# Three products at a time taken from VectorE's last scans by GpSimd, between its gathers, and a second accumulator bank

## What is computed

```python
# mamba branch (d_inner 512, 16 states)
xz = xn @ in_proj.T;  x, z = split(xz);  x = silu(causal_conv4(x) + conv_b)
dt, Bm, Cm = split(x @ x_proj.T);  dt = softplus(dt @ dt_proj.T + 2 * dt_proj_b)
h[t] = exp(dt * A) * h[t-1] + dt * Bm[t] * x[t]          # 16 states for each of 512 channels
y = (sum over states of h * Cm + x * D) * z;  return y @ out_proj.T
# moe branch: 64 experts, the 8 best of each token, hidden 256, inner 128
h = silu(x @ w1_e.T) * (x @ w3_e.T);  out += weight * (h @ w2_e.T)
```

## Time and profile before

| | us |
|---|---|
| three runs | 499.99, 503.32, 513.6 |
| median | 503.32 |
| the profiled execution | 495.79 |
| its span on the core | 494.0 |
| VectorE busy in the span | 432.0 (87%) |
| TensorE busy | 410.0 (83%) |
| GpSimd busy | 327.0 (66%) |
| ScalarE busy | 248.2 (50%) |
| mean granted TensorE clock | 0.906 |

### The profile page before, as it was taken

One profiled execution on the slowest core, in us unless ns is written; L12 is line 12 of the kernel. 1 busy time (PEld: TensorE's weight loads), 2 busy tenths in 40 slices (PEclk: granted clock), 3 DMA queues, 4 the chain that ended last, 5 costly groups with the idle time before them and its releaser, 6 DMA issues. The chain is left out here.

```text
span 494.0 us, 8730 instructions
## 1 busy us (share of the span) xinstructions
PE 410.0 (83%) x2094; PEld 299.1 (61%) x2094; DVE 432.0 (87%) x651; ACT 248.2 (50%) x469; POOL 327.0 (66%) x281
## 2 busy tenths in 40 slices
PE   1986989018859999899999998899989849865997
PEld 1732434002229888788978886788878735533675
DVE  5297999989997998999889997999899899999984
ACT  1245269132335566566666674556656522554560
POOL 2000578777767788878865665878877687778770
PEclk9997899655558999999999998999999988995999
DMA  8999389962234999999999996999999663333331
GB/s 274 428 425 426 138 297 400 407 244 106 101 144 159 347 376 374 354 322 357 346 365 329 338 359 234 347 340 353 363 349 336 247 202 93 101 113 105 113 117 53
DMA packets 51849, 134.39 MB, mean 272 GB/s; under 512 B 7120, under 2 KB 11216, under 8 KB 49776
## 3 DMA queue, kind: packets, MB, share of 16 engines
q1 hardware_dynamic: 45680, 117.31, 65.1%
q0 software_dynamic: 6144, 16.79, 10.3%
HBM read 90.49 MB, written 45.68 MB: 276 GB/s over the span
## 5 line engine op out<-in xcount | busy, mean ns | idle before, releaser
L344 POOL TENSOR_TENSOR dbu<-dtu,bc 128x512 f32 x80 | 102.7, 1286 | 57.3 <-DVE bank L600 46.4
L336 POOL DMA_INDIRECT slot_x<-x_sb,slot x64 | 69.3, 1082 | 68.5 <-DMA slot_x<-bc 49.3
L600 DVE TENSOR_TENSOR_SCAN bank<-dA,dbu 128x512 f32<-128x512 f32 x68 | 92.6, 1362 | 8.9 <-POOL dbu L344 1.3
L786 ACT ACTIVATE dA<-dt_sb,a_neg 128x512 f32<-128x512 f32 (+1 forms) x68 | 49.2, 725 | 68.2 <-DVE bank L600 68.1
L600 DVE TENSOR_TENSOR_SCAN bank<-bank,dbu 128x512 f32<-128x512 f32 x60 | 73.7, 1229 | 5.3
L1034 PE MATMUL bank<-x_sb,wring 128*128 128x128 f32 x528 | 67.9, 284 | 0.0
L606 DVE TENSOR_TENSOR hc<-bank,bc 128x512 f32<-128x512 f32 x90 | 61.8, 687 | 5.2 <-POOL hp L354 3.2
L1034 PEld LDWEIGHTS bank<-x_sb,wring 128*128 128x128 f32 x528 | 65.0, 200 | 0.3
L1034 PE MATMUL bank<-x_sb,xw 128*128 128x128 f32 x512 | 62.6, 275 | 0.7 <-DMA xw<-w_moe 0.7
L1034 PEld LDWEIGHTS bank<-x_sb,xw 128*128 128x128 f32 x512 | 59.7, 192 | 1.2 <-issue 1.2
L786 ACT ACTIVATE bank<-dt_sb,a_neg 128x512 f32 x60 | 41.6, 693 | 35.1 <-DVE bank L600 35.0
(11 more groups left out here) (175 smaller groups left out, 735.8 us busy)
## 6 DMA issues: line engine op xcount, KB each, us to landing
xw<-w_moe SPq DMA_DIRECT2D x64, 384.0 KB, 5.4
wring<-w_moe SPq DMA_DIRECT2D x64, 384.0 KB, 5.4
slot_y<-x_sb SPq DMA_DIRECT2D x66, 256.0 KB, 5.5
slot_x<-bc SPq DMA_DIRECT2D x16, 1024.0 KB, 21.9
bc<-bc_dram SPq DMA_DIRECT2D x8, 1024.0 KB, 15.5
xg<-slot_x SPq DMA_DIRECT2D x16, 512.0 KB, 6.0
xw<-slot_x SPq DMA_DIRECT2D x16, 512.0 KB, 6.1
slot_y<-w_moe SPq DMA_DIRECT2D x1, 2048.0 KB, 13.7
```

The source lines that it names most:

```text
L336: pool.indirect_dma_start(slot_x, bass.IndirectOffsetOnAxis(ap=slot[:, t * K + k:t * K + k + 1], axis=0), x_sb[:, t, :], None).then_inc(sc ...
L344: nc.gpsimd.tensor_tensor(dbu[:, j], at(dtu, g), bc[:, bass.ds(n, 1), 0].rearrange("p a l -> p (a l)"), ALU.mult).then_inc(dbu_ok, 1)
L600: nc.vector.tensor_tensor_scan(H[:], dA[:, j] if fall is None else fall, dbu[:, j], 0.0, ALU.mult, ALU.add).then_inc(scan_ok, 1)
L786: nc.scalar.activation(dA[:, j] if fall is None else fall, at(dt_sb, g), ACT.Exp, scale=a_neg[:, bass.ds(g, 1), bass.ds(n, 1)].rearrange(" ...
```

## The change

Four parts.

1. GpSimd leaves group 5 after its state 11. The products `spread_u` of states 12 to 15 of group 5 are made by VectorE, `times_c` of these states writes four buffers of their own (`hc_alone`), and TensorE adds them one by one with `sum_states`; GpSimd makes neither their products nor their `add_pair`.
2. GpSimd's 64 gathers start after that, and are interrupted twice: in front of gather 22 it makes the products of states 13, 14, 15 of group 6, in front of gather 44 those of states 10, 11, 12 of group 7. They go to four buffers `extra`; VectorE makes no `spread_u` for these six states and reads `extra` in the scan.
3. Group 6 is summed in a bank of its own (`PS[1]`); group 7 in `Y_ACC`, whose first sum then waits for `finish_group` of group 5. `finish_group` of group 6 now stands behind six states of group 7. The table `PROJ` and the output banks are laid out anew.
4. The SBUF reserved for GpSimd's DMA descriptors (`dynamic_dma_scratch_size`) is set to 8192 bytes a partition, where it had its default of 16384; `extra` takes 8 KB a partition.

```diff
+        extra = sb("extra", [P, 4, L])
+        hc_alone = [f[:].rearrange("p t e -> p (t e)") for f in (prob, key)] + [
+            wx[:].rearrange("p t n -> p (t n)")[:, 0:L], hp[:]]
-        OUT = [PS[i][:, 0:DM] for i in (4, 5, 6, 7, 1, 2, 4, 5)]
+        OUT = [PS[i][:, 0:DM] for i in (4, 5, 6, 7, 2, 4, 5, 6)]
-        PROJ = {9: (4, 0), 11: (4, 1), 13: (5, 0), 15: (5, 1), 21: (6, 0), 23: (6, 1), 25: (7, 0), 26: (7, 1),
-                27: (4, 2), 28: (5, 2), 29: (6, 2), 30: (7, 2)}
+        PROJ = {9: (4, 0), 10: (4, 1), 20: (5, 0), 21: (5, 1), 24: (6, 0), 25: (6, 1), 26: (4, 2), 27: (5, 2),
+                28: (7, 0), 29: (7, 1), 30: (6, 2), 31: (7, 2)}
+        def acc_of(g):
+            return PS[1] if g == G2 else Y_ACC
+        ALONE = NS - 4
+        PAUSE = {22: ((G2, 13), (G2, 14), (G2, 15)), 44: ((G3, 10), (G3, 11), (G3, 12))}
+        BY_POOL = [s for group in PAUSE.values() for s in group]
...
-            with pool.Fori(DT, G2) as g:
+            with pool.Fori(DT, G2 - 1) as g:
                 with pool.Fori(0, QG // 2) as q:
                     pairs(g, q)
-            add_pair((G2 - G1) * QG - 1, 1)
+            with pool.Fori(0, ALONE // 4) as q:
+                pairs(G2 - 1, q)
+            r = (G2 - 1 - G1) * QG + ALONE // 2 - 1
+            add_pair(r, 1)
+            def ahead(g, n):
+                i = BY_POOL.index((g, n))
+                if i >= 4:
+                    pool.wait_ge(scan_ok, BY_POOL[i - 4][0] * NS + BY_POOL[i - 4][1] + 1 + C)
+                nc.gpsimd.tensor_tensor(extra[:, i % 4], dtu[:, g], bc[:, n, 0], ALU.mult).then_inc(dbu_ok, 1)
...
                 for k in range(K):
+                    for g, n in PAUSE.get(t * K + k, ()):
+                        ahead(g, n)
                     pool.indirect_dma_start(
...
-            def light(g, p):
+            def light(g, p, alone=False):
...
                         scan(g, n, k % 2, dA_light(n))
+                        if alone and ALONE - 1 <= n < NS - 1:
+                            spread_u(g, n + 1, 1 - k % 2)
...
+            light(G2 - 1, (G2 - GH - 2) * LIGHT + V_LAST, alone=True)
...
+            def tail_pair(g, q):
+                for j in range(2):
+                    n = 2 * q + j
+                    if n % PART == 0 and (n >= RING or g == G3):
+                        dve.wait_ge(acc_ok, g * NS + n - RING + PART + C)
+                    s = (g - G2) * NS + n
+                    if (g, n) in BY_POOL:
+                        i = BY_POOL.index((g, n))
+                        dve.wait_ge(dbu_ok, DBU_MOE + i + 1)
+                        scan(g, n, j, given=extra[:, i % 4])
+                    else:
+                        dve.wait_ge(dbv_ok, NS + NS - ALONE + s + 1 - sum((h - G2) * NS + m < s for h, m in BY_POOL))
+                        scan(g, n, j)
+                    after = (g, n + 1) if n < NS - 1 else (g + 1, 0)
+                    if after[0] < G and after not in BY_POOL:
+                        spread_u(after[0], after[1], 1 - j)
+                    times_c(g, n, j, hc_end)
...
-                if n == 0:
-                    pe.wait_ge(y_out, g + 1)
+                if n == 0 and g == G2:
+                    pe.wait_ge(scan_ok, G2 * NS + C)
+                elif n == 0:
+                    pe.wait_ge(y_out, min(g + 1, G2 + 1))
...
-            sum_quad((G2 - G1) * (NS // 4) - 1)
+            for n in range(ALONE, NS):
+                sum_states(G2 - 1, n, hc_alone, 1)
...
-    nc = bacc.Bacc("TRN2", target_bir_lowering=False, num_devices=1)
+    nc = bacc.Bacc("TRN2", target_bir_lowering=False, num_devices=1, dynamic_dma_scratch_size=8192)
```

More of the change, by code:

```diff
@@ L594, in spread_u, with scan @@
                                         ALU.mult).then_inc(dbv_ok, 1)
-            def scan(g, n, j, fall=None):
+            def scan(g, n, j, fall=None, given=None):
                 s = g * NS + n
@@ L599, in scan @@
                 dve.wait_ge(hc_ok, s + C)
-                nc.vector.tensor_tensor_scan(H[:], dA[:, j] if fall is None else fall, dbu[:, j], 0.0, ALU.mult, ALU.add).then_inc(scan_ok, 1)
+                nc.vector.tensor_tensor_scan(H[:], dA[:, j] if fall is None else fall, dbu[:, j] if given is None else given, 0.0, ALU.mult, ALU.add).then_inc(scan_ok, 1)
             def times_c(g, n, j, ring=None):
@@ L607, in times_c, with finish_group @@
                                         ALU.mult).then_inc(hc_ok, 1)
-            def finish_group(g):
+            def finish_group(g, bank=None):
                 dve.wait_ge(acc_ok, (g + 1) * NS + C)
-                nc.vector.scalar_tensor_tensor(at(u_g, g), at(u_g, g), at(d_col, g), Y_ACC[:], ALU.mult, ALU.add).then_inc(y_out, 1)
+                nc.vector.scalar_tensor_tensor(at(u_g, g), at(u_g, g), at(d_col, g), (bank or Y_ACC)[:], ALU.mult, ALU.add).then_inc(y_out, 1)
                 dve.wait_ge(y_out, g + 2)
@@ L656, in light @@
                         n = 4 * c + k
-                        dve.wait_ge(dbu_ok, (g - G1) * NS + n + 1)
+                        own = alone and n >= ALONE
+                        if own:
+                            dve.wait_ge(dbv_ok, NS + n - ALONE + 1)
+                        else:
+                            dve.wait_ge(dbu_ok, (g - G1) * NS + n + 1)
                         scan(g, n, k % 2, dA_light(n))
+                        if alone and ALONE - 1 <= n < NS - 1:
+                            spread_u(g, n + 1, 1 - k % 2)
                         if k in (0, 3):
                             hidden(p + 3 * c + (0 if k == 0 else 2), (3 * c + (0 if k == 0 else 2)) % 2)
-                        if k % 2 == 0:
-                            dve.wait_ge(hp_ok, (g - G1) * QG + n // 2 + 1)
-                        times_c(g, n, k % 2)
+                        if own:
+                            if n == NS - 1:
+                                dve.wait_ge(hq_ok, (G2 - G1) * (NS // 4))
+                            times_c(g, n, k % 2, hc_alone)
+                        else:
+                            if k % 2 == 0:
+                                dve.wait_ge(hp_ok, (g - G1) * QG + n // 2 + 1)
+                            times_c(g, n, k % 2)
                         if k == 1:
@@ L1001, in sum_states @@
                 pe.wait_ge(hc_ok, g * NS + n + C + 1)
-                if n == 0:
-                    pe.wait_ge(y_out, g + 1)
-                mm = nc.tensor.matmul(Y_ACC[:], ident[:], ring[n % len(ring)], start=(n == 0), stop=True, skip_group_check=True)
+                if n == 0 and g == G2:
+                    pe.wait_ge(scan_ok, G2 * NS + C)
+                elif n == 0:
+                    pe.wait_ge(y_out, min(g + 1, G2 + 1))
+                mm = nc.tensor.matmul(acc_of(g)[:], ident[:], ring[n % len(ring)], start=(n == 0), stop=True, skip_group_check=True)
                 if count:
```

35 lines of the change are left out of this document (15 added, 20 removed).

## The result

The changed kernel took 512.76 us (median of 4 executions, 511.14 to 514.34) against 507.28 for the kernel before beside it (499.99 to 513.6); the ratio is 1.0221 [1.0142, 1.03]. It is slower, by 2.2% with an interval from 1.4 to 3.0, and the time lies outside the predicted range. Medians here are over all executions, and the ratios leave out those that lie over 1.5% above the fastest of their kernel, so a ratio is not always the quotient of the medians beside it.

What follows compares the result with a forecast made beforehand. VectorE and TensorE were taken to share the end. VectorE's last `times_c`, 480.1 + 1.9 - 0.8 - 2.7 + 5.4 = 483.9 us, plus the path behind gave span 494.7, forecast 504.0 us; 8-in-10 range 497.5 to 508.5.

Steps and rivals of the forecast that it cites:

- So the gathers start 10.3 us earlier: Part 1: GpSimd, free after state 11 of group 5, issues its first gather near 386.8 us instead of 397.10.
- 0.59 + 0.46 + 0.24: Part 1: costs to VectorE of added `spread_u` in group 5, within a sum of 1.9 us for four.
- the scan's -0.8: First scan of group 6: 1.23 us instead of 2.02, as GpSimd's last `add_pair` no longer runs beside it.
- I take 0: Part 4: halving the descriptor space costs the 64 gathers nothing, out of a possible 0 to 4.3 us.
- the forecast -3.1 us: Part 3, kernel's end: TensorE's last sum follows VectorE's last `times_c` sooner, one projection added; the end moves -3.1 us.
- both lock orders: Part 2: GpSimd gets the SBUF port also between scan and `spread_u` (494.7 us), or only behind both (496.2 us).
- Rival 2: Last tile's eight products wait for the last gather, so gathers end last: beyond 496.2, to 500.5 us; chance 0.12.
- the gathers' path: From first gather at 386.8 us through 64 gathers and two trios to 492.2 us, 2.5 short of the bound.
- the waits on `cb_ok` ... don't bind: Gathers 32 to 63 never wait for TensorE's combines; gather 56 comes near 473 us, its combine near 462.
- Rival 1: Groups 6 and 7: GpSimd's six products are nearly free for VectorE; span 489.3 us, time 498.5; chance 0.27.
- Rival 3: Kernel's end: part 3 fails, TensorE idles and its clock falls to 0.50, adding 2 to 3 us (497.7); chance 0.06.
- granted clock 1.00 from 420 us to the end: Sign for part 3 in the changed profile: TensorE stays at full clock, 2.4 GHz, from 420 us on.

Runs made afterwards that it cites:

- b_again: The kernel before, unchanged, run again on chip 3 with a second profile: 502.37 us, ratio 0.9999.
- s_ring16: The changed kernel with the default descriptor space of 16384 bytes and `extra` placed in `z_sb`, on chip 8: 497.72 us, ratio 1.0041.
- c_drain5: a_notrio with GpSimd waiting for all issued gathers before gathers 4, 8, 12, 32 and 48 (from 0), on chip 7: 493.58 us, ratio 0.9977.
- a_notrio: a_ring16 without the six products on GpSimd, so VectorE makes them and the gathers are unbroken, on chip 3: 509.0 us, ratio 1.0132.
- b_bank: The kernel before with part 3 alone, on chip 3: 510.45 us, ratio 0.9992.
- f_drain5: The program of c_drain5, run on chip 0b beside f_after: 499.7 us, ratio 0.9894.
- after: The changed kernel with all four parts, its first measurement and profile, chip not recorded: 512.76 us, ratio 1.0221.
- a_again: The changed kernel, unchanged, run again on chip 0 with a second profile: 510.01 us, ratio 1.019.
- a_ring16: The changed kernel with the default descriptor space of 16384 bytes and `extra` placed in `z_sb`, on chip 0: 510.8 us, ratio 1.0217.
- f_after: The changed kernel, unchanged, run once more on chip 0b: 513.4 us, ratio 1.017.
- a_hold: The changed kernel with GpSimd's first gather held until ScalarE's last tanh of the experts, on chip 0: 506.53 us, ratio 1.0123.
- a_drain4: a_ring16 with GpSimd waiting ahead of every fourth gather until all issued ones have landed, on chip 3: 532.7 us, ratio 1.0536.
- b_ring8: The kernel before with only the descriptor space set to 8192 bytes, on chip 0: 504.03 us, ratio 1.0075.

## Why the prediction was wrong

**The step that failed is in part 1**, at "So the gathers start 10.3 us earlier". I counted that as room for the gathers and nothing else. What runs between 387 and 397 us is the experts' last pair, a chain from TensorE to ScalarE to VectorE and back with one increment at each step. The stream of gathers held up TensorE's increment for 16.1 us, and the distance grew by 15.4 where 1.3 was forecast (0.59 + 0.46 + 0.24; the first of the four `spread_u` lies ahead of it, and the scan's -0.8 behind). Take the standstill away and the forecast is near: 15.38 - 14.41 = 0.97. The experts' last pair does stand in the prediction's last paragraph, as something that would make it wrong, but for the reason that their weights share the DMA engines; the DMA share was 0.32 to 0.56 during the standstill, and the products in question had been computed. The trace of before gave a hint that I didn't follow: its own median lay 1.5% above the profiled execution, which I carried over as a factor. b_again shows some of what lay in it, waits for late increments of 4.70 and 3.16 us that come and go with the chip. Where nothing is held up the forecast of the ratio is close: 1.0014 for the whole change, 1.0041 in s_ring16, which leaves out part 4.

**Part 4**, "I take 0", was wrong by a pause of 2.6 us, and in another place than I looked. It costs nothing in the stream of 64 gathers, and 2.6 us at the 57th scatter.

**Part 3**: the forecast -3.1 us is what c_drain5 shows (12.82 against 15.87), in a kernel where no other path ends last. That kernel has part 1 too, and part 3 alone was not run on such a chip. a_notrio has 12.83 on a chip with hold-ups, so they don't always hide it; in b_bank nothing is to be seen of it. In the changed kernel only -1.56 is left, as the gathers end last.

**Part 2**: 0.8 us a product for VectorE by the rows, where 0.9 was taken, and +2.6 to +3.3 us on the stretch, where +2.7 was; both lock orders occur. One trio goes through as a block of 3.78 us with VectorE's instruction waiting for all of it, the other takes turns, 5.47 us. s_ring16 is the clean test of the sum: VectorE's last `times_c` ends at 483.6, and 483.9 was forecast. That they lie 0.3 us apart is in part luck: state 12 of group 5 was scanned 1.10 us later than before, of which 0.59 was forecast, and from there on VectorE took 2.4 us more, where 3.2 was.

**Rival 2 came true**, to which I gave 0.12: "the gathers become the end". In s_ring16 its span is 496.4, where the gathers' path was put at 492.2. The 4.2 us are three mis-sized terms. The first gather went out at 387.6 and not 386.8 (+0.8). The stream took 98.5 us and not 96.7 (+1.8): the trios were shorter than thought, 9.4 us of pauses instead of 12.4, but five gathers took 1.78 to 1.79 us, and one, the thirty-third, waited 2.4 us for a combine. So "the waits on `cb_ok` ... don't bind" was wrong as well: little here, 9.69 us in the changed kernel's own profile. And the last tile began 3.6 us after the last gather's instruction ended, where the earlier trace rows gave 1.85 (+1.7). The margin of "2.5 us short of being the bound" was smaller than the sum of such errors.

**Rival 1** is refuted (0.8 us a product, not nothing). **Rival 3**: TensorE's first sum of group 7 has no idle time worth naming, but "granted clock 1.00 from 420 us to the end" does not hold, though 448 to 452 us are at 1.00: it is 0.76 from 436 to 440 us in the changed kernel, 0.50 from 424 to 428 in s_ring16. Neither was late on the path that ended last.

**What stays open**: what it is in the chip that holds increments up. All those that cost VectorE over 2 us here are TensorE's. They are late on some chips (0, 3 and 0b; before takes 501 to 505 there, and 494 to 495 on 7 and 8), and only beside GpSimd's streams of indirect DMAs or in the 7 us behind one. An unbroken stream isn't enough: the changed kernel's runs on from 417 us, broken three times, and nothing is over 0.5 us late. Nor must the stream stop for an increment to come, as f_drain5 shows at 84 us. On those chips the profiler's records of increments are also incomplete, 6270 to 7094 of about 8500, on the other two complete; and what is missing is missing in the same two stages, beside scatters and gathers (from 120 to 130 us the changed kernel's trace has 25 records and s_ring16's 142, from 160 to 380 us they agree within 1%). Every execution that I can look into is profiled. So a strong rival is untested: that recording the increments is what delays them, and that the kernel unprofiled has no hold-up. Whether the lost records are the sign or the cause, these runs can't tell. What they show is the order on the chips with hold-ups, without an exception at the experts' end: an unbroken stream and the standstill (after, a_again, a_ring16, a_notrio, f_after); the stream later or broken, and none (a_hold, a_drain4, f_drain5).

## What to carry over

When an edit lets a long stream of transfers from GpSimd start earlier, list the semaphore hand-overs that will then lie beside it, above all chains through TensorE, and break the stream there: waits for landed gathers ahead of the 5th, 9th and 13th took away some 13 us of standstill here (on two of four chips; on the others there was none) and left GpSimd idle for 7 to 8. A baseline profile that is 1.5% faster than the median of its runs is not the whole baseline: take a second one before the terms of a sum are read from it. And compare stretches of two profiles with the spread between executions in mind: the first stretch took 387.03, 385.41 and 383.89 us in three profiles of one and the same program. And when the path that ends last is shortened by 3 us, the next path needs its margin worked out with the landing time of its last transfer as it is then, not as it is now.

## What the runs showed of the hardware

- TensorE's semaphore increments arrived up to 16.1 us after the work (after, 396.66 to 412.79) while GpSimd issued a gather each 1.25 us, and 2.3 to 3.9 us after the stream stopped (a_hold, after, b_again). Beside scatters one came 3.9 us late with the stream running on (f_drain5). In some such stretches TensorE itself runs one matmul in 2.1 us (b_again, b_bank).
- It depends on the chip: one and the same program was at 1.0217 of before on one and at 1.0041 on another. On chips 7 and 8 none of eight profiles has an increment of TensorE over 0.3 us late, on 0, 3 and 0b all ten have.
- A descriptor space of 8192 instead of 16384 makes GpSimd pause 2.6 us ahead of the 57th scatter, in the changed kernel and in before alike (after, a_again, a_hold, b_ring8, f_after).
- Three GpSimd products back to back can keep VectorE's two-input instruction out for all of them (3.23 us for one of 0.69); the port is not always handed over between them.
- A break in the stream (waiting until all issued gathers have landed) leaves GpSimd idle for 2.0 to 3.4 us, where 0.3 is usual between two gathers.
